# Output gate and values emptied at the end of a turn, behind all exponentials, with the scores of the next batch waiting for them

## The reference

```python
mod = (_silu(c) @ wmod).reshape(8, 6, 1, -1)          # sa, ca, ga, sb, cb, gb
ga = (2 * (ga >= 0) - 1) * jnp.maximum(jnp.abs(ga), 0.25)
h = _layernorm(x) * (1 + ca) + sa
g = log_sigmoid(h @ gk_w1 @ gk_w2 + gk_b) / 16
o = scan(S = exp(g)[:, None] * S + k[:, None] * v[None, :];  o = q @ S)     # per head
o = o * rsqrt(mean(o * o) + EPS) * rms_w
x = x + ga * ((o * silu(h @ Wg)) @ Wo)
h = _layernorm(x) * (1 + cb) + sb
probs = softmax(h @ router_w.T); vals, idx = top_k(probs, 2)
x = x + gb * sum_e w_e * (gelu(h @ w1[e].T) @ w2[e].T)
```

## Time and profile before

| | us |
|---|---|
| median of 3 runs | 484.72 |
| runs | 484.72, 577.58, 480.71 |
| the profiled execution, its own time | 475.34 |
| its span, first to last instruction | 473.6 |
| busy in the span: PE, DVE, ACT, POOL | 373.6, 294.6, 262.8, 162.9 |
| start of the transposed norm HT of batches 0, 1, 2, 7 (ACT L486) | 11.35, 40.83, 72.32, 239.99 |
| first matmul of an expert block (PE L1253) | 293.21 |
| first transpose of the late blocks (PE L1236) | 360.47 |

### The profile page before, as it was taken

How to read it: one execution, slowest core, us unless ns; L and a number is a source line. 1 busy time by engine, 2 the same in 40 slices (tenths; PEclk the granted TensorE clock), 3 DMA queues, 4 the chain that set the end, 5 groups by cost and what they waited for, 6 DMA issues and landing times. The chain is left out here.

```text
span 473.6 us, 8504 instructions
## 1 busy us (share of the span) xinstructions
PE 373.6 (79%) x2362; PEld 310.5 (66%) x2363; DVE 294.6 (62%) x839; ACT 262.8 (55%) x570; POOL 162.9 (34%) x215
## 2 busy tenths in 40 slices
PE   3939699699699689687796865978998999999700
PEld 2227387386476546655664755978998999999600
DVE  3684776796797786877967956354563334344067
ACT  3583655846846937747657513564755565656200
POOL 4000000033051060060050140338578888876700
PEclk9979969889889799799799777988999999999855
DMA  7920000000000010010010012122244323221087
GB/s 232 286 105 2 0 0 1 1 19 28 1 30 17 2 39 6 0 45 0 0 45 2 6 51 47 51 55 65 67 136 124 90 75 89 61 80 35 8 320 211
DMA packets 27522, 28.80 MB, mean 61 GB/s; under 512 B 4413, under 2 KB 22224, under 8 KB 27360
## 3 DMA queue, kind: packets, MB, share of 16 engines
q1 hardware_dynamic: 22944, 19.92, 14.2%
q0 software_dynamic: 4544, 8.47, 5.4%
HBM read 16.62 MB, written 12.67 MB: 62 GB/s over the span
## 5 line engine op out<-in xcount | busy, mean ns | idle before, releaser
L418 POOL TENSOR_TENSOR PadP<-Id 128x1 f32<-128x1 f32 x47 | 11.3, 240 | 225.9 <-DVE SlotI L929 191.6
L1267 PE MATMUL ps<-W,G 128*128 x624 | 76.9, 277 | 0.0
L1267 PEld LDWEIGHTS ps<-W,G 128*128 128x128 f32 x624 | 74.3, 195 | 0.0
L430 POOL DMA_INDIRECT expert_rows<-HR,SlotI x64 | 63.8, 996 | 21.5 <-issue 21.2
L441 POOL DMA_INDIRECT expert_out<-YS,Ids x62 | 64.7, 1044 | 18.6 <-issue 16.4
L601 ACT ACTIVATE G<-ps 128x512 f32<-128x512 f32 x78 | 46.4, 599 | 12.5 <-PE ps L1255 7.5
L1253 PE MATMUL ps<-XThi,W1b 128*128 128x256 f32 x156 | 48.9, 314 | 4.1 <-DVE XTlo L1015 3.9
L1009 DVE CAST W1b<-W 128x1024 fp32r x39 | 27.6, 707 | 36.8 <-PE ps L1255 30.5
L1255 PE MATMUL ps<-XThi,W1b 128*128 128x256 f32 x156 | 45.4, 291 | 0.0
L1254 PE MATMUL ps<-XTlo,W1b 128*128 128x256 f32 x156 | 45.4, 291 | 0.0
L773 DVE TENSOR_TENSOR PT<-ps,Causal 128x512 f32<-128x512 f32 x32 | 21.8, 681 | 28.9 <-PE ps L1128 28.9
(11 more groups left out here) (206 smaller groups left out, 756.9 us busy)
## 6 DMA issues: line engine op xcount, KB each, us to landing
XR<-expert_rows SPq DMA_DIRECT2D x39, 130.0 KB
Y<-expert_out SPq DMA_DIRECT2D x8, 512.0 KB, 7.0
W<-in_w1T SPq DMA_DIRECT2D x1, 2048.0 KB, 10.6
W<-in_w2T SPq DMA_DIRECT2D x1, 2048.0 KB, 8.0
out<-X SPq DMA_DIRECT2D x8, 256.0 KB, 3.9
expert_rows<-PadRow SPq DMA_DIRECT2D x9, 130.0 KB, 2.5
expert_rows<-HR,SlotI POOLq DMA_INDIRECT x64, 2.3
expert_out<-YS,Ids POOLq DMA_INDIRECT x62
```

The source lines that it names most:

```text
L430: nc.gpsimd.indirect_dma_start(rows_dram, bass.IndirectOffsetOnAxis(ap=SlotI[u][:, k, c:c + 1], axis=0), HR[u][:, k, c, :], None, bounds_c ...
L1267: ins = mm(bank_y(j, r)[:, half * D:(half + 1) * D], G[r % 2][:, k, t], w2, start=(k == 0), stop=(k == KH - 1))
```

## The change

The two square brackets of a turn on ScalarE are moved. The exponentials, QB and the root of the norm come right after the second square; then the silu table, the two copies of transposed O, the four values and gates, and the exp table. The four chunks of values go into four banks, `pjA`, `pjB`, `psS0` and `psS1`; the scores of the next batch, which use `psS0` and `psS1`, now wait until all four are emptied (`vg`). O is transposed into `psK` and `psO`. The row of gates is spread into the free quarter of `psK`, ahead of the transposes of the end keys; the piece `modulation` is gone, `WoB` is formed from `psK`, behind `ket` (ScalarE's copy of the end keys), and stands on VectorE right behind the addition to `X`. On VectorE the routing's softmax goes behind slots and statistics; in the drain the table of early blocks and several pieces change place.

```diff
+        def bank_values(c):
+            return (pjA, pjB, psS0, psS1)[c]
+        def bank_out(b, j):
+            return (psS0 if last(b) else psK, psO)[j]
...
+            def silu_table(b, u):
+                nc.scalar.preload_act_table_set("silu_and_others")
             def values(b, u, chunks):
-                if 0 in chunks:
-                    nc.scalar.preload_act_table_set("silu_and_others")
...
-                "p3_logits-1 p2_output23+0 p1_values01+1 p1_values23+1 p2_rms+0 "
-                "p1_differences+1 p1_decays+1 p2_transpose0+0 p2_transpose1+0 p1_starts+1 p3_rank-1 "
-                "p1_keys+1 p3_back-1"),
+                "p3_logits-1 p2_output23+0 p1_differences+1 p1_decays+1 p1_starts+1 p1_keys+1 p2_rms+0 p1_silu+1 "
+                "p2_transpose0+0 p2_transpose1+0 p1_values01+1 p1_values23+1 p3_rank-1 p3_back-1"),
...
             def gated_wo(b, u):
-                wait(dve, "rows_ps", b + 1)
+                wait(dve, "ket", b + 1)
                 wait(dve, "at_ps", b)
-                v.tensor_tensor(WoB[:], Wo[:], psT[:, 0:D]...
+                v.tensor_tensor(WoB[:], Wo[:], psK[:, 3 * P:4 * P]...
...
-                "p1_stats+1 p2_mask0+0 p2_wob+0 p1_norm+1 p2_mask1+0 p2_state+0 p2_out01+0 p3_norm-1 "
+                "p1_stats+1 p2_mask0+0 p1_norm+1 p2_mask1+0 p2_state+0 p2_out01+0 p3_norm-1 "
                 "p2_mask2+0 p2_mask3+0 p1_loggates+1 p1_sums+1 "
-                "p1_differences+1 p2_out23+0 p2_squares+0 p1_diffq+1 p3_logits-1 p2_rms+0 p1_keys01+1 p1_keys23+1 p1_qe+1 "
-                "p3_rank-1 p1_keysend+1 p3_counts-1 p1_qs+1 p2_project+0 p3_softmax-1 p3_slots-1 p3_stats+0 p2_silu+1"),
-                     "p2_mask0:7 p2_wob:7 p2_mask1:7 table p2_state:7 p2_out01:7 p3_norm:6 p2_mask2:7 p2_mask3:7 p2_out23:7 "
+                "p1_differences+1 p1_diffq+1 p2_out23+0 p1_qe+1 p2_squares+0 p1_keys01+1 p2_rms+0 p1_keys23+1 p2_silu+1 "
+                "p3_logits-1 p3_rank-1 p1_keysend+1 p3_counts-1 p1_qs+1 p2_project+0 p2_wob+1 p3_slots-1 p3_stats+0 p3_softmax-1"),
+                     "p2_mask0:7 p3_norm:6 p2_mask1:7 p2_state:7 p2_out01:7 p2_mask2:7 table p2_mask3:7 p2_out23:7 "
...
             def values(b, u, c):
-                    wait(pe, "vg", C * b + c - 1)
-                mm((pjA, pjB)[c % 2][:], ...
+                    wait(pe, "pt", C * b + c - 3)
+                mm(bank_values(c)[:], ...
             def score(b, u, c):
-                    wait(pe, "oT", 2 * b)
+                    wait(pe, "vg", C * b + C)
+                    wait(pe, "ktil", (NS + 1) * b + NS)
             def scores(b, u):
+                wait(pe, "oT", 2 * b)
+                pe.wait_ge(s["rows_fin"], 1)
+                wait(pe, "silu_b", b + 1)
+                mm(psK[:, 3 * P:4 * P], PickB[:], RowsAll[:, 0, :], start=True, stop=True)
                 for c in range(3):
                     ins = nc.tensor.transpose(psK[:, c * P:(c + 1) * P], KE[:, c, :], Id[:])
-            def modulation(b, u):
...
             def state(b, u):
+                wait(pe, "wo_b", b + 1)
...
-                "p1_values2+1 p1_values3+1 p3_back-1 p2_transpose+0 p2_project+0 p2_keysT+1 p3_rank-1 "
-                "p2_score0+1 p2_score1+1 p2_rows+1 p2_state+1 p2_chunk0+1"),
+                "p3_back-1 p2_transpose+0 p2_project+0 p2_score0+1 p2_score1+1 p2_keysT+1 p3_rank-1 p2_state+1 p2_chunk0+1"),
```

More of the change, by code:

```diff
@@ L525, in values @@
                     wait(act, "vg_ps", C * b + c + 1)
[L526 to L527 removed]
+                    nc.scalar.copy(VG[:, c, :], bank_values(c)[:, 0:DV])
+                    nc.scalar.activation(Sg[u][:, c, :], bank_values(c)[:, DV:], ACT.Silu).then_inc(s["vg"], 1)
                 if C - 1 in chunks:
@@ L574, in output_transpose @@
                 wait(act, "oT_ps", 2 * b + j + 1)
-                nc.scalar.copy(OT[:, j, :], ((psS0, psO) if last(b) else (psS0, psS1))[j][:]).then_inc(s["oT"], 1)
+                nc.scalar.copy(OT[:, j, :], bank_out(b, j)[:]).then_inc(s["oT"], 1)
             def logits(b, u):
@@ L644, in _ @@
                      p1_keycopy=keys_copy, p1_loggates=log_gates, p1_values01=part(values, range(0, 2)),
-                     p1_values23=part(values, range(2, 4)), p1_differences=differences, p1_decays=decays,
+                     p1_values23=part(values, range(2, 4)), p1_silu=silu_table, p1_differences=differences, p1_decays=decays,
                      p1_starts=decays_start, p1_keys=keys,
@@ L776, in scores @@
             def scores(b, u):
-                wait(dve, "rows_ps", b)
+                wait(dve, "ket_ps", b)
                 v.tensor_copy(PickB[:], Id[0:B, bass.ds(b, 1)].to_broadcast([B, P])).then_inc(s["silu_b"], 1)
@@ L1081, in transpose @@
                 wait(pe, "xhat1", C * b + C)
-                wait(pe, "wo_b", b)
+                wait(pe, "slot", b - 2)
                 for c in range(C):
@@ L1153, in scores @@
                 ins.then_inc(s["ket_ps"], 1)
-            def modulation(b, u):
-                pe.wait_ge(s["rows_fin"], 1)
-                wait(pe, "silu_b", b + 1)
-                wait(pe, "slot", b - 1)
-                if isinstance(b, int) and b == EARLY + 1:
-                    wait(pe, "cnt_sb", 1)
-                mm(psT[:, 0:D], PickB[:], RowsAll[:, 0, :], start=True, stop=True).then_inc(s["rows_ps"], 1)
             def state(b, u):
@@ L1175, in output_transpose @@
                 wait(pe, "pt", C * b + C)
-                for j, ps in enumerate((psS0, psO) if last(b) else (psS0, psS1)):
+                wait(pe, "s_tmp", 2 * b + 2)
+                for j in range(2):
                     for c in range(C):
-                        ins = nc.tensor.transpose(ps[:, c * P:(c + 1) * P], O[:, c, j * P:(j + 1) * P], Id[:])
+                        ins = nc.tensor.transpose(bank_out(b, j)[:, c * P:(c + 1) * P], O[:, c, j * P:(j + 1) * P], Id[:])
                     ins.then_inc(s["oT_ps"], 1)
@@ L1195, in logits @@
                     wait(pe, "hT", b + 3)
-                wait(pe, "wo_b", b + 2 if not isinstance(b, int) or b < B - 1 else B)
+                if isinstance(b, int) and b >= EARLY:
+                    wait(pe, "slot", b)
+                if isinstance(b, int) and b == EARLY:
+                    wait(pe, "cnt_sb", 1)
                 for c in range(C):
@@ L1291, in _ @@
                      p1_values3=part(values, 3), p2_keysT=scores, p2_score0=part(score, 0), p2_score1=part(score, 1),
-                     p2_rows=modulation, p2_state=state, p2_chunk0=part(chunk, 0), p2_chunk1=part(chunk, 1),
+                     p2_state=state, p2_chunk0=part(chunk, 0), p2_chunk1=part(chunk, 1),
                      p2_score2=part(score, 2), p2_score3=part(score, 3), p2_chunk2=part(chunk, 2),
```

12 lines of the change are left out of this document (5 added, 7 removed), and 2 rows, old and new, of the table ins.

## The result

The changed kernel takes 510.74 us (median of 4 runs, 509.14 to 512.54); the kernel before, run with it, 482.72 (median of 4 runs). Single runs of a kernel fall into a slower state, 577.58 among them, and the ratio, 1.0618 with a 95% interval of [1.0508, 1.0729], is taken without those, against a mean of 481.04 us: slower. The profiled execution took 509.14 us with a span of 507.4 and a mean granted clock of 0.860.

The account below looks back on a forecast made before the run. No engine is full; waits between engines bound a turn, decided ahead of ScalarE's root and between projection and Xh. 475.3 + 5.4 + 14.4 + 9.6 + 2.6 - 4.0 = 503.3, plus 4.7 gives 508 us; range 491 to 520.

Parts of the forecast that it names:

- The total: Whole kernel: 503.3 us on the profiled execution, plus 4.7, half its 9.4 gap to the median, gives 508.
- What bounds a turn: No engine full; ScalarE's work ahead of the root and VectorE's own queue from X to Xh decide a 33.68 us turn.
- Ahead of the root: On ScalarE, exponentials and QB replace table loads and values, 6.0 us; the root gains only about 0.15 us.
- The values hidden: ScalarE's values at their new place end before TensorE's projection does, with 0.4 to 1.0 us of cover.
- Rival (c): ScalarE's values end last and hold up the scores; 1 us beyond cover in each of seven turns: 515; chance 0.05.
- The wait at WoB: VectorE, behind the addition to X, waits 2.7 us for ket; a turn is 2.4 us longer, 14.4 over six.
- The clock in the new hole: TensorE idles 3.4 us behind the state, then runs at half speed: 1.6 us a turn, 9.6 over six.
- Rival (a): VectorE's stall of 2.4 us a turn comes, but TensorE's clock holds over the hole: 493.7, or 498; chance 0.26.
- The first turn: Table and values delay batch 0's scores to near 36.6, Xh of batch 1 to 43.8: +5.4 us.
- Last turn and drain: Batch 6's turn has the same stall, +2.6 us; the drain to the first expert matmul gets shorter, -4.0.
- The shift carried to the end unchanged: Early and late expert blocks hang on the drain in one chain, so expert work adds 0 us.
- Rival (b): Transposes of O and projection run at full clock; a turn loses 0.75 us: 482.2, or 487, no change; chance 0.09.

Follow-up runs that it names:

- F1: Kernel before the change, with 28 unread identity transposes on TensorE ahead of the transposes of O, except the last batch; 472.92 us, ratio 0.9889.
- F2: Changed kernel with 24 unread identity transposes behind the state and 28 ahead of the transposes of O on TensorE; 482.96 us, ratio 1.0097.
- G2: G1 with 14 unread identity transposes behind the state and 28 ahead of the transposes of O on TensorE; 466.72 us, ratio 0.977.
- G1: Changed kernel with end keys and routing sums ahead of the scores on TensorE, second norm's statistics ahead of WoB on VectorE; 471.71 us, ratio 0.986.
- E1: Changed kernel with WoB back behind the next batch's first mask on VectorE, slots given a wait for earlier scatters; 504.64 us, ratio 1.0562.
- E4: Changed kernel with 24 unread identity transposes on TensorE behind the state, ahead of the first output chunk; 502.45 us, ratio 1.0503.
- E3: Changed kernel with gate row, end keys' transposes and routing sums ahead of the scores on TensorE; 484.86 us, ratio 1.015.

## Why the prediction was right, point by point

The forecast of 508 us for 510.74 rests on the mechanism that was named, and the experiments bear it out; single terms of the sum were mis-sized, in both directions, and that the total came so close is in part luck.

- **The total.** On the profiled execution the sum gave 503.3 us, and 509.14 was measured: 5.8 were missing. The 4.7 added for the median stood in for most of them. It was half of a gap of 9.4 us between three runs of the kernel before, one of them of 577.58, and its profiled execution (475.34). After the change that gap is 1.6 us, and over the later runs of the kernel before it is 2.3 (477.61): the closeness of 508 to 510.74 owes something to this allowance, not to the mechanism.
- **What bounds a turn.** Right in the turns that it was read from. F1 shows it from the other side: with TensorE faster between O and X, VectorE's queue still sets the time.
- **Ahead of the root.** An exchange without gain, as predicted: with both holes filled (F2, G2), HT to root takes 17.1 to 17.2 us in the last four turns against 17.3 to 17.4 before. In the changed kernel the root is later, 19.2 us in the turn shown, behind key gates and queries at half speed; root to X, which the sum left unchanged, gives 2.5 us back over six turns.
- **The values hidden.** Right, with more cover than I had thought: 2.3 us instead of up to 3.41, because all four banks are full when ScalarE comes, and it is done 1.6 us before the projection ends. Rival (c) is refuted for this kernel. The cover was the slow projection: in F2, with the projection in 2.02 us, the scores wait 0.34 us for the last gate in four of the six turns.
- **The wait at WoB.** 2.7 us predicted; 2.56 measured in four of the six turns, 3.55 and 3.47 in two, together 17.3 where 16.2 were predicted. The 1.9 us beyond 2.56 in the two are a size that I missed: I took the scores at 2.03 us as in the earlier trace rows, but the slow stretch behind the old hole falls later than before and reaches into them (3.02 us). From the addition to X to Xh the six turns grow by 18.2, 0.9 more than the wait: VectorE's rearranged queue is itself a little longer there, as G1 shows without a wait (35.6 against 34.2); I had reckoned it shorter by the 0.11 of PickB. E1 adds what I had not said: had WoB not waited, the slots would have, on the same list of TensorE.
- **The clock in the new hole.** The size: 9.6 predicted, 9.7 by E4, 7.7 after what is given back; the hole is 3.29 us long in the turn shown (3.4 predicted), with 0.50 behind it. The place was wrong, and the size came out partly by luck. I had the 1.6 us a turn on the way to HT, in the chunk and Xh's transposes; only 2.5 us of the six-turn sum lie there (in the turn shown the chunk, from 232.93 for 1.97, runs beside Xh on VectorE, from 232.90 for 1.11), and 7.3 lie behind HT, in key gates and queries, which I had taken as untouched. Rival (a), the stall without the clock, is refuted by the 0.50 in the stretch from 233 to 242.
- **The first turn.** Xh at 43.8 predicted, 44.18 measured, through scores at 35.96 (36.6 predicted). The first output chunk and Xh's transposes behind it then ran at half speed, which the sum had not counted for this turn: +6.8 instead of +5.4. E3 and G1, with the end keys ahead of the scores, bring the first turn back to 32.0 and 31.5 us, so most of it is a matter of order too.
- **Last turn and drain.** +2.6 and -4.0 predicted, +4.8 and -2.7 measured. The 20.39 us from the first mask to the first expert matmul lie in the 18 to 21 that were named. The last turn was under-sized: the wait at WoB is 3.71 us there, and HT to X is 0.8 us longer.
- **The shift carried to the end unchanged.** Not quite: the expert work came out 2.9 us shorter. Over the kernels profiled here that part lies between 177.5 and 180.5 us, with no relation to the edits that I can see (F1, with expert work as before, 177.7); I do not know its cause.
- **Rival (b)**, a projection at full clock that makes the change neutral: it did not happen by itself, but F2, which forces it together with a filled second hole, gives nearly its time: 483.28 us in the profiled execution, where (b) had 482.2, with 1.15 us lost a turn instead of 0.75.

## What to carry to other kernels

When an operation at the head of an in-order queue gets a new operand, look up where that operand's producer stands in its own engine's list, and move the producer or put independent work ahead of the consumer; E3 and G1 turn a loss of 6% into 1.4% less than the kernel before by two such moves. A wait also costs what the idle engine loses behind it: here some 10 us of clock beside 17 us of waiting. The other way round, a slow stretch that lay beside other work can come to cost time when the order changes: filling the hole ahead of the transposes of O gave 1.15 us over six turns in the kernel before, where the clock fell elsewhere in return, and 12.8 in the changed one. Where a hole cannot be closed, work without a reader can hold TensorE's clock, but pays little where another engine's queue ends last. In the last five turns of the kernel before, VectorE waits at most 0.29 us for the projection, and F1 gains nothing in them; in G1 it waits 0.77 to 1.27, and the filling (G2) takes that away.

## What the runs showed of the hardware that I had not expected

- The half-speed stretch does not end when TensorE is busy again: 9 us at 0.50 with TensorE busy for all 9.00 of them in the changed kernel, and 16 us in a turn of E3, behind holes of 3.29 and 2.71 us. In the kernel before, the first operation at half speed starts at 225.65 and the clock is 1.00 again from 232 on the earlier trace rows.
- The same idle time, 3.5 to 3.6 us ahead of the transposes of O, is followed by half speed at once (1.97 us) or only in the work behind them (1.18 us, then a projection of 3.75). Shorter holes went either way. In F1, 1.88 us of idle time ahead of the row of gates came before a state at full speed in one turn (1.56 us) and at half speed in another (2.84). In G1 the chunk was at full speed behind holes of 1.84, 1.91 and 2.27 us and slower behind 1.78 and 1.86 (1.57 and 1.68 us instead of 1.1). So in these runs the length of such a hole alone does not tell whether the clock falls.
- Emptying values and gates takes ScalarE 2.3 us for four pairs when no bank has to be waited for, against 3.41 in the kernel before.
